# Causal mask by row tiles of 32 columns, and a new order of steps, in the first attention stage of a two-layer gated model

## The chip, the core and the metric

One Trainium2 chip, of which the program uses one core. The core has TensorE (matmuls, 128x128 array, 32-row or 32-column tiles of it can be used by themselves), VectorE, ScalarE and GpSimd, and SyncE, whose queue issues all DMAs here. The engines run their own instruction streams and meet at semaphores. The metric is the device time of one execution in microseconds.

## The reference

Two layers of gated cross attention and gated feed-forward, on x of 8 batches x 256 rows x 512. Each stage adds its result, times the tanh of a gate, to x. Only what the change touches is spelled out:

```python
# stage A: 16 heads of 32; key and value are both the context; causal
scores = jnp.einsum('bhqd,bhkd->bhqk', q, kj) * SCALE
scores = jnp.where(k_off > q_idx, -jnp.inf, scores)
exp_c = jnp.exp(scores - scores.max(axis=-1, keepdims=True))
out = jnp.einsum('bhqk,bhkd->bhqd', exp_c / exp_c.sum(-1, keepdims=True), vj)
...
x = x + jnp.tanh(g_xattn[0]) * _L0_xattn_ref(_layernorm(x), ctx, ctx)
x = x + jnp.tanh(g_ffn[0])   * _L0_ffn_ref(_layernorm(x), w_gate_up, w_proj)   # ternary weights, groups of 64
x = x + jnp.tanh(g_xattn[1]) * _L1_xattn_ref(_layernorm(x), ctx, q_w, ..., norm_k_img_w)
x = x + jnp.tanh(g_ffn[1])   * _L1_ffn_ref(_layernorm(x), w_norm, w_gv, w_out) # ternary weights, one scale
```

## The kernel before

X, the state of all eight batches, lies in on-chip memory from first to last. The work is in stages: A (L0 attention), B (L0 feed-forward, with products `b_gate_up` and `b_project`), and then C and D interleaved (L1 attention and L1 feed-forward). The change touches stage A and the step into stage B.

Stage A takes a batch per turn, in eight turns, as a software pipeline written out by hand for each engine. In a turn TensorE does this for batch b, with e = b-1 (its end) and f = b+1 (its front):

- `a_scores(b, g)`, g = 0..3: the scores of four heads, query rows on partitions, in banks 0 to 3. First the mask: one matmul per bank of the identity (128x128, bf16) with the mask (0 or -1e30, `maskS`), 256 columns, which fill the two diagonal corners of the bank. Then the products of queries and keys (L428), in four 32-row tiles, one head in each. VectorE reduces each group to maxima (L1339, `a_scores`). After two groups `a_max_parts` splits them into two bf16 parts (`a_mhl`), TensorE turns them (`a_max_turn`, L437) and VectorE copies the rows (`a_max_rows`, L1355, `a_mtr`).
- `a_probs(b, g)`: the same scores with keys on partitions, in banks 4 to 7: mask (`maskT`, L450), products (L454), and the maxima subtracted by a matmul with a selector (L459). ScalarE takes the exponential (L987).
- `a_weigh` and `a_sum` (L475, L487): the weighted values and the sums, in 32-column tiles, banks 4 and 5, for two groups at a time ("half"). `a_turn_sums`, `a_turn_out` and `a_turn_x` (L412) are transposes; VectorE divides and adds to X (`a_divide`, `a_add_out`), normalises (`stats`, `normed`), ScalarE copies the turned x to QT (`a_queries`).
- `a_project(turn, b, i)`, i = 0..3 (L517, L520): keys and values of L1 for the same context, f32, four matmuls and for the keys a bias; ScalarE copies them out, SyncE stores them to device memory.
- `a_group_sum` (L528): sums of the magnitudes of L0's feed-forward weights over groups of 64, three units a turn, banks 2 and 3. ScalarE makes magnitudes and signs before it (`a_signs`) and means after it (`a_group_mean`), VectorE rounds to ternary (`a_distance`, `a_ternary`, and for the first 16 units a maximum, L1403). `a_abs_sum` on ScalarE gathers the magnitudes of L1's weights.

Eight banks are shared by `Ring`: each has a list of who uses it in a turn, and `freed(name, turn)` gives the semaphore that the user before raises. After the turns, `m_weights` (L612, L614) spreads a maximum and sums over partitions, for which VectorE makes `m_in` at the end of its last turn (L1484); its results set the scales that the second `b_gate_up` waits for. Turn 0 (the start) loads constants, x, keys and weights in SyncE's order, makes the first projections and turns x.

The ring of bank 1, as an example of what a later step waits for:

```python
Ring([banks[1]], scores_of(0) + [("ot2", s.a_otr, 3, 0, 2)] + scores_of(2) + kv[1]),
```

Of the kernel before, what the change touches and what calls it, by code (L numbers as in the profile page):

```python
# [6 lines left out]
ALU = mybir.AluOpType  # L7
ACT = mybir.ActivationFunctionType
F32 = mybir.dt.float32
# [29 lines left out]
    ld_cst ld_x0 ld_x1 ld_kt0 ld_kt1 ld_rv0 ld_rv1 ld_w00 ld_w01 ld_w02 ld_w1a ld_w1b ld_wk ld_wv ld_sel ld_wqo ld_kb ld_row ld_wn  # L39
# [108 lines left out]
def build(nc, x, ctx, ctxT, gates, w0, w1, wkv, wqo, vec, wnorm, cols, cst, selq, selc, out):  # L148
    with ExitStack() as stack:
# [16 lines left out]
        def area(a, plan):  # L166
# [6 lines left out]
                           ("block", (P,), BF16), ("maskS", (P,), BF16), ("maskT", (P,), BF16), ("selq", (2, P), BF16), ("count", (2, DH), F32),  # L173
# [5 lines left out]
        pre = area(W0[:, :].bitcast(F32), [("cst", (4 * P,), F32), ("selq", (2 * P,), F32), ("selc", (4 * P,), F32)])  # L179
# [19 lines left out]
        late = 1  # L199
        def scores_of(first):  # L200
            return [(f"sc{g}", s.a_scr, 4, g, late) for g in (first, first + 1)]

        def probs_of(j, first):
            return [(f"pr{g}", s.a_ex, 16, 4 * g + j, late) for g in (first, first + 1)]
# [7 lines left out]
                 Ring([banks[4]], [("pv1", s.a_pvr, 2, 1, 2)] + probs_of(0, 0) + [("pv0", s.a_pvr, 2, 0, late)] + kv[0] + probs_of(0, 2)),  # L212
# [3 lines left out]
        bank_of_kv = (4, 1, 6, 7)  # L216
# [71 lines left out]
        def sync_program(sp):  # L288
# [120 lines left out]
        def tensor_program(pe):  # L409
# [7 lines left out]

            def a_scores(b, g):
                QT, KT = (bufA[n][:, b % 2 * KD + g, :] for n in ("QT", "KT"))
                pe.wait_ge(s.a_xtr, 2 * b + 2)  # L420
                pe.wait_ge((s.ld_kt0, s.ld_kt1)[b % 2], 16 * (b // 2 + 1))
                for j in range(4):
                    pe.wait_ge(*ringA[j].freed(f"sc{g}", b + 1))
                for j in range(4):
                    pe.matmul(corners(banks[j]), keep["identb"], doubled(bufA["maskS"]), start=True, stop=False, skip_group_check=True)
# [14 lines left out]
            def a_probs(b, g):  # L440
# [3 lines left out]
                if (b, g) == (0, 0):  # L444
                    pe.wait_ge(s.const, 2)
                if (b, g) == (NB - 1, 2):
                    pe.wait_ge(s.b_xl, 2)
                for j in range(4):
                    pe.wait_ge(*ringA[4 + j].freed(f"pr{g}", b + 1))
                    pe.matmul(corners(banks[4 + j]), keep["identb"], doubled(bufA["maskT"]), start=True, stop=False, skip_group_check=True)  # L450
# [5 lines left out]
                for kb in range(TB):  # L456
                    at, q0 = kb * S, kb * P
                    for j in range(4):
# [50 lines left out]
            def a_project(turn, b, i):  # L509
                what, t = i // TB, i % TB  # L510
                bank = banks[bank_of_kv[i]]
# [3 lines left out]
                pe.wait_ge(*ringA[bank_of_kv[i]].freed(f"kv{i}", turn))  # L515
# [15 lines left out]
            pe.wait_ge(s.const, 1)  # L531
            def b_turn_x(f):
                for t in range(TB):
# [3 lines left out]
                    else:  # L537
                        to = banks[6 + t]
                        pe.wait_ge(*ringA[6 + t].freed(f"xt{t}", NB))
# [3 lines left out]
            def b_gate_up(b, p, parts=(0, 1)):  # L543
# [11 lines left out]
                for part_ in parts:  # L555
                    bank, col, done = banks[first + part_], part_ * HID + 2 * p * P, (s.b_g, s.b_gu)[part_]
                    for i in range(2):
# [4 lines left out]
                    mm.then_inc(done, 1)  # L562

            a_project(0, 0, 0)
# [1518 lines left out]
```

## Time and profile before

| | us |
|---|---|
| median of 3 runs | 1184.49 (1184.33 to 1187.55) |
| the profiled execution | 1191.87 |
| its span | 1190.1 |
| TensorE busy, matmuls | 1125.8 (95%) |
| VectorE busy | 831.8 (70%) |
| ScalarE busy | 567.5 (48%) |
| start to scores 0 of turn 1 | 26.3 |
| turns 1 to 8, to the second gate product | 26.3 to 336.0 |

The span is the stretch from the first to the last instruction in the hardware's trace. A row of the timeline gives the start and the length of a run of like instructions; a matmul's length includes its way through the array, so a row of matmuls reaches past the start of the next. What a group costs TensorE is the distance from its start to the start of the next group. A number in brackets is idle time of the engine, with what ended it. Line numbers are those of the kernel before; of the changed kernel they are its own.

### The profile page before, as it was taken

The numbers are of one execution on the slowest core, as the hardware profiler recorded it, in microseconds if no ns is written. First come the engines' busy times: TensorE is split into PE (matmuls) and PEld (weight loads), VectorE is DVE, ScalarE is ACT, GpSimd is POOL, SyncE is SP. The second block draws the span as 40 slices with busy tenths as digits, with TensorE's granted clock in tenths as the row PEclk, the third lists the DMA queues.
The fourth block names the chain that finished last, engine by engine and source line by source line (L and its number), as shares of the span: only waits on it lengthen the run. The fifth ranks groups of instructions, "written<-read, shape, count | busy, mean of one in ns | idle before, by whom it ended". The sixth has DMA issues, their size and how long they took to land.

```text
span 1190.1 us, 23943 instructions
## 1 busy us (share of the span) xinstructions
PE 1125.8 (95%) x9578; PEld 686.0 (58%) x9672; DVE 831.8 (70%) x1440; ACT 567.5 (48%) x918; POOL 74.1 (6%) x180
## 2 busy tenths in 40 slices
PE   5899999999899999999999999899999999999998
PEld 2455555555577777777777655445454545454543
DVE  3677777666866765755666566778787878777785
ACT  3565666656443332333333343437373737372654
POOL 0000000000000000000000110110101010101010
PEclk9999999999999999999999999999999999999899
DMA  8554445441321201111101021000101010100000
GB/s 298 201 170 138 142 139 187 161 130 67 107 63 36 63 19 36 54 36 36 54 19 36 18 81 37 3 35 20 35 6 49 2 53 2 36 11 10 10 10 36
DMA packets 28973, 78.75 MB, mean 66 GB/s; under 512 B 3008, under 2 KB 3136, under 8 KB 28480
## 3 DMA queue, kind: packets, MB, share of 16 engines
q1 hardware_dynamic: 28864, 77.22, 19.8%
q8 instruction: 78, 1.28, 0.5%
q14 instruction: 31, 0.25, 0.1%
HBM read 64.63 MB, written 12.58 MB: 65 GB/s over the span
## 4 chain that ended last, share of the span: by engine, by line
PE 81%; DVE 9%; issue 4%; ACT 3%; another core or an unknown queue 2%; DMA 0%; SPq 0%; POOL 0%; ACTq 0%; DVEq 0%; POOLq 0%
PE bank L560 9%; PE bank L561 9%; PE bank L648 9%; PE bank L628 9%; PE bank L751 8%; PE bank L517 6%; PE bank L739 5%; PE bank L412 5%; PE bank L781 5%; DVE ARENA L1339 3%; PE bank L720 3%; PE bank L701 3%; PE bank L454 2%; PE bank L428 2%
## 5 line engine op out<-in xcount | busy, mean ns | idle before, releaser
L560 PE MATMUL bank<-ARENA,W 128*128 128x256 f16 x1024 | 228.6, 274 | 0.9 <-issue 0.9
L561 PE MATMUL bank<-ARENA,W 128*128 128x256 f16 x1024 | 228.7, 274 | 0.0
L956 ACT ACTIVATE ARENA<-bank 128x512 f32<-128x512 f32 (+3 forms) x143 | 92.8, 688 | 117.8 <-PE bank L412 39.2
L517 PE MATMUL bank<-ARENA 128*128 128x512 f32 x256 | 121.6, 620 | 10.6 <-DMA ARENA<-in_wkv 9.8
L751 PE MATMUL bank<-W,ARENA 128*128 128x512 bf16 x493 | 116.9, 383 | 2.5 <-issue 0.7
L628 PE MATMUL bank<-W,ARENA 128*128 128x512 bf16 x472 | 114.8, 379 | 3.1 <-DVE ARENA L1371 0.9
L648 PE MATMUL bank<-ARENA 128*128 128x512 f32 x256 | 116.8, 599 | 0.0
L560 PEld LDWEIGHTS bank<-ARENA,W 128*128 128x128 bf16 x1024 | 100.6, 98 | 19.7 <-issue 1.2
L561 PEld LDWEIGHTS bank<-ARENA,W 128*128 128x128 bf16 x1024 | 100.5, 98 | 18.4
L1519 DVE SCALAR_TENSOR_TENSOR ARENA<-bank,ARENA 128x512 f32<-128x512 f32 x64 | 48.0, 750 | 79.3 <-PE bank L561 78.2
L956 ACT ACTIVATE ARENA<-ARENA 128x512 f16<-128x512 f32 x64 | 40.3, 630 | 130.9 <-DVE ARENA L1519 128.1
L1144 ACT ACTIVATE ARENA<-bank,ARENA 128x512 f32<-128x512 f32 x64 | 43.7, 685 | 113.8 <-PE bank L751 106.5
L1339 DVE TENSOR_REDUCE ARENA<-bank 128x4 f32<-128x512 f32 x64 | 58.2, 951 | 52.1 <-PE bank L428 52.1
L1933 POOL TENSOR_TENSOR ARENA<-ARENA 128x2 f32<-128x2 f32 (+1 forms) x72 | 48.8, 677 | 722.4 <-DVE ARENA L1329 479.7
L751 PEld LDWEIGHTS bank<-W,ARENA 128*128 128x128 bf16 x512 | 49.1, 99 | 66.6 <-issue 12.3
L517 PEld LDWEIGHTS bank<-ARENA 128*128 128x128 f32 x256 | 48.6, 197 | 65.1 <-issue 54.0
L1065 ACT ACTIVATE ARENA<-bank 128x512 f32<-128x512 f32 x64 | 38.2, 596 | 99.1 <-PE bank L561 99.0
L1590 DVE RECIPROCAL ARENA<-bank 128x256 f32<-128x256 f32 x32 | 56.2, 1757 | 37.4 <-PE bank L739 37.3
L1559 DVE TENSOR_REDUCE ARENA<-bank 128x4 f32<-128x1024 f32 x64 | 75.2, 1218 | 6.7 <-PE bank L701 6.7
L628 PEld LDWEIGHTS bank<-W,ARENA 128*128 128x128 f16 x512 | 49.9, 99 | 49.4 <-issue 2.8
L1525 DVE TENSOR_TENSOR ARENA<-ARENA 128x512 f16<-128x512 f32 x64 | 44.3, 692 | 47.2 <-ACT ARENA L956 47.2
L648 PEld LDWEIGHTS bank<-ARENA 128*128 128x128 f32 x256 | 46.6, 190 | 52.3 <-issue 51.2
(178 smaller groups left out, 1801.5 us busy)
## 6 DMA issues: line engine op xcount, KB each, us to landing
W<-in_w SPq DMA_DIRECT2D x48, 512.0 KB, 3.8
ARENA<-in_w SPq DMA_DIRECT2D x24, 512.0 KB, 3.6
kv_store<-ARENA SPq DMA_DIRECT2D x32, 256.0 KB, 3.1
W<-kv_store SPq DMA_DIRECT2D x15, 512.0 KB, 4.5
X<-in_x SPq DMA_DIRECT2D x8, 512.0 KB, 4.7
ARENA<-in_ctxT SPq DMA_DIRECT2D x8, 512.0 KB, 3.8
ARENA<-in_ctx SPq DMA_DIRECT2D x8, 512.0 KB, 4.4
out<-X SPq DMA_DIRECT2D x16, 256.0 KB, 3.0
```

Source lines behind the costliest of these rows:

```text
L412: mm = pe.transpose(to[:, k * P:(k + 1) * P], tile, one)
L517: mm = pe.matmul(bank, bufA["KT"][:, b % 2 * KD + k, t * P:(t + 1) * P], W[:, k, :], start=(k == 0), stop=(k == KD - 1 and what == 1))
L560: pe.matmul(bank[:, i * S:(i + 1) * S], W0[:, at:at + P], xt_half(b, 0)[:, k, :], start=(k == 0), stop=False)
L561: mm = pe.matmul(bank[:, i * S:(i + 1) * S], W0[:, at:at + P], xt_half(b, 1)[:, k, :], start=False, stop=(k == KD - 1))
L628: mm = pe.matmul(banks[6 + t], hx(q, what)[:, i * S + t * P:i * S + (t + 1) * P], W0[:, UP_AT + m * D:UP_AT + (m + 1) * D], start=(m == 0 ...
L648: pe.matmul(to, src[:, k, t * P:(t + 1) * P], WQ[w][:, k, :], start=(k == 0), stop=False)
L739: mm = pe.matmul(part(to, j)[:, what * S:(what + 1) * S], lhs, bufC["PT"][:, h % 8, kb * S:(kb + 1) * S], start=(kb == 0), stop=True, skip ...
L751: mm = pe.matmul(to, QQ[d][:, t, k * P:(k + 1) * P], W1[:, at:at + D], start=(k == 0), stop=(k == KD - 1))
L781: mm = pe.matmul(to, UT[d, t][:, k * P:(k + 1) * P], W1[:, UP_AT + k * D:UP_AT + (k + 1) * D], start=(k == 0), stop=(k == KH - 1))
L956: return act.activation(to, src, ACT.Copy)
L1339: got = v.tensor_reduce(NM[:, t, :, g % 2], bank[:, 0:4, t * P:t * P + (t + 1) * P], AX_X, ALU.max, negate=True)
L1559: got = v.tensor_reduce(NM[:, t, :, g], bank[:, 0:4, t * S:(t + 1) * S], AX_X, ALU.max, negate=True)
```

## The change

Parts:

1. The mask matmul is cut into strips. `a_mask` puts four strips of 32 mask columns (twice, for the two corners: 64 columns) into each of four banks, each strip with a matmul that uses 32 rows of the array: the stationary operand is a 32 x 128 part of the mask, stored in another layout (`maskS`, `maskT` are now 4 x 128 per partition, loaded as `masks`, 512 KB, by a DMA of its own), the moving one a 32 x 32 part of the identity, read twice. 16 matmuls of 64 columns instead of 4 of 256, for each of the 64 blocks.
2. TensorE's order in a turn is new; ScalarE's and VectorE's follow. `project(b,3)` moves ahead of the group sum of unit 1, `project(f,0)` ahead of probs 1, the turning out and `a_weigh(b,0)` between scores 2 and 3; VectorE does distance and ternary of unit 1 ahead of the reduction of scores 2. Key and value products 0 and 1 both use bank 1, and the exponentials go through banks 6, 7, 4, 5 in this order.
3. The start: keys, weights of the key projection and the bias come first in SyncE's queue, x and constants after. VectorE makes `ones` and zeros first, TensorE runs ten matmuls on zeros, then both key products of batch 0, then the transposes. VectorE splits the bias before it takes x's statistics.
4. The last turn: stage B's first transposes go to banks 1 and 0 and stand between probs 0 and probs 1, the first gate products are split in halves (`sides`), and `m_weights` stands ahead of probs 3. `b_project` of batch 0 waits for as many ternary units as it needs, not for all.

```diff
+def strip(bank, m):
+    return corners(bank)[:, :, m * DH:(m + 1) * DH]
...
-                 Ring([banks[1]], scores_of(0) + [("ot2", s.a_otr, 3, 0, 2)] + scores_of(2) + kv[1]),
+                 Ring([banks[1]], scores_of(0) + [("ot2", s.a_otr, 3, 0, 2)] + kv[0] + scores_of(2) + kv[1]),
...
-            sp.dma_start(pre["cst"], cst).then_inc(s.ld_cst, 16)
-            load_x(0)
             load_keys(0)
...
+            load_x(0)
+            sp.dma_start(pre["cst"], cst).then_inc(s.ld_cst, 16)
...
+            sp.dma_start(pre["masks"], masks).then_inc(s.ld_sel, 16)
...
+            def a_mask(to, mask):
+                for m in range(4):
+                    for j in range(4):
+                        one = part(keep["identb"], j)[:, j * DH:(j + 1) * DH]
+                        pe.matmul(strip(to[j], m), part(mask, j)[:, m, :], doubled(one), start=(m == 0), stop=False, skip_group_check=True)
...
-                for j in range(4):
-                    pe.matmul(corners(banks[j]), keep["identb"], doubled(bufA["maskS"]), start=True, stop=False, skip_group_check=True)
+                a_mask(banks[0:4], bufA["maskS"])
...
+                if (b, g) == (NB - 1, 2):
+                    pe.wait_ge(s.b_xl, 2)
...
+            for n in range(10):
+                pe.matmul(banks[7], bufA["MHL"][:, 0, :], bufA["MHL"].rearrange("p a b -> p (a b)"), start=True, stop=True)
+            a_project(0, 0, 0)
+            a_project(0, 0, 1)
+            pe.wait_ge(s.const, 2)
+            a_turn_x(0, 0)
...
+                a_scores(b, 1)
+                if end:
+                    a_sum(turn, e, 1)
+                    a_project(turn, b, 3)
+                a_group_sum(turn, b, 1)
+                a_max_turn(turn, b, 0)
+                if end:
+                    a_turn_sums(turn, e)
+                a_probs(b, 0)
+                a_group_sum(turn, b, 2)
+                if front:
+                    a_project(turn, f, 0)
+                else:
+                    b_turn_x(0)
+                a_probs(b, 1)
+                a_scores(b, 2)
+                if end:
+                    a_turn_out(turn, e)
+                a_weigh(turn, b, 0)
+                a_scores(b, 3)
+                a_sum(turn, b, 0)
...
+                    m_weights()
+                    b_gate_up(0, 0, (1,), (0,))
+                a_probs(b, 3)
...
                 if back:
+                    a_distance(b, 1)
+                    if not front:
+                        b_turn_x(0)
+                    a_ternary(b, 1)
                     a_scores(b, 2)
-                    a_distance(b, 1)
```

How the instructions stand. On TensorE in the middle of an ordinary turn (turn 5), from the mask of scores 1 (L425 before, L433 after) to the turning of the sums (L412, L423). Before:

```order
L425 MATMUL bank<-ARENA 128x2x128 x4
L428 MATMUL bank<-ARENA 128x128 x4
L428 MATMUL bank<-ARENA 128x256 x4
L487 MATMUL bank<-ARENA 32x256 x4
L487 MATMUL bank<-ARENA 32x128 x4
L487 MATMUL bank<-ARENA 32x256 x4
L487 MATMUL bank<-ARENA 32x128 x4
L528 MATMUL bank<-W,ARENA 128x512 x2
L517 MATMUL bank<-ARENA 128x512 x4
L437 MATMUL bank<-ARENA 128x128 x2
L528 MATMUL bank<-W,ARENA 128x512 x2
L412 MATMUL bank<-ARENA,W 128x128 x4
```

After (L537 is the projection, L548 the group sum, L457 the turning of the maxima):

```order
L433 MATMUL bank<-ARENA 128x2x32 x16
L448 MATMUL bank<-ARENA 128x128 x4
L448 MATMUL bank<-ARENA 128x256 x4
L505 MATMUL bank<-ARENA 32x256 x4
L505 MATMUL bank<-ARENA 32x128 x4
L505 MATMUL bank<-ARENA 32x256 x4
L505 MATMUL bank<-ARENA 32x128 x4
L537 MATMUL bank<-ARENA 128x512 x4
L548 MATMUL bank<-W,ARENA 128x512 x2
L457 MATMUL bank<-ARENA 128x128 x2
L423 MATMUL bank<-ARENA,W 128x128 x4
```

The projection has moved ahead of the group sum, the second group sum is gone from here (it comes after probs 0), and the mask's matmuls are 16 narrow ones.

On SyncE at the start of the program, before:

```order
L323 DMA W<-in_cst 128x512
L292 DMA X<-in_x 128x2x512
L298 DMA ARENA<-in_ctxT 128x1024
L326 DMA ARENA<-in_gates 128x4
L327 DMA ARENA<-in_cols 128x12
L328 DMA ARENA<-in_wkv 128x2048
L329 DMA ARENA<-in_vec 128x512
```

After (the first four rows are keys, key weights, bias and x):

```order
L308 DMA ARENA<-in_ctxT 128x1024
L334 DMA ARENA<-in_wkv 128x2048
L335 DMA ARENA<-in_vec 128x512
L302 DMA X<-in_x 128x2x512
L337 DMA W<-in_cst 128x256
L338 DMA ARENA<-in_gates 128x4
L339 DMA ARENA<-in_cols 128x12
L320 DMA W<-in_w 128x1024
L341 DMA ARENA<-in_wkv 128x2048
L342 DMA W<-in_masks 128x1024
```

Keys, weights and bias come before x and the constants; the masks are a load of their own behind the value weights.

On TensorE at the end of turn 8, from the mask of probs 3, before (L612 and L614 are `m_weights`):

```order
L450 MATMUL bank<-ARENA 128x2x128 x4
L454 MATMUL bank<-ARENA 128x256 x4
L454 MATMUL bank<-ARENA 128x128 x4
L459 MATMUL bank<-ARENA 128x256 x4
L459 MATMUL bank<-ARENA 128x128 x4
L612 MATMUL bank<-W,ARENA 32x128 x4
L614 MATMUL bank<-ARENA 32x24 x4
```

And after, from the mask of probs 2 (L589 and L591 are `m_weights`, L579 and L580 a gate product):

```order
L433 MATMUL bank<-ARENA 128x2x32 x16
L472 MATMUL bank<-ARENA 128x256 x4
L472 MATMUL bank<-ARENA 128x128 x4
L477 MATMUL bank<-ARENA 128x256 x4
L477 MATMUL bank<-ARENA 128x128 x4
L589 MATMUL bank<-W,ARENA 32x128 x4
L591 MATMUL bank<-ARENA 32x24 x4
L579 MATMUL bank<-ARENA,W 128x256
L580 MATMUL bank<-ARENA,W 128x256
```

`m_weights` has moved from behind probs 3 to right behind probs 2, and a quarter of the first gate products follows it.

## Rows read from the trace of the kernel before

**Rows 1.** The page: busy time and share by engine; the chain's shares.

```profile
PE 1125.8 (95%) x9578; PEld 686.0 (58%) x9672; DVE 831.8 (70%) x1440; ACT 567.5 (48%) x918; POOL 74.1 (6%) x180
...
PE 81%; DVE 9%; issue 4%; ACT 3%; another core or an unknown queue 2%; DMA 0%; SPq 0%; POOL 0%; ACTq 0%; DVEq 0%; POOLq 0%
```

**Rows 2.** Windows: stretch: us, busy us (instructions) per engine, granted clock, DMA share, GB/s.

```profile
9.80:13.20 3.40, 3.37 (x4) 1.51 (x5) 2.35 (x8) 0.00 (x0) 0.69 (x1) 1.00 1.05 422
37.20:40.50 3.30, 3.30 (x6) 1.24 (x5) 1.34 (x5) 2.91 (x3) 0.69 (x1) 0.50 0.48 170
54.00:282.00 228.00, 216.00 (x2292) 124.28 (x2303) 164.47 (x282) 140.98 (x246) 4.14 (x6) 1.00 0.46 147
```

**Rows 3.** Timeline of TensorE, turns 2 to 4: start, us, instructions [idle before <-releaser].

```profile
65.02 0.61 PE L425 MATMUL bank<-ARENA 128*128 128x256 bf16 x4
...
140.92 0.34 PE L459 MATMUL bank<-ARENA 32*128 32x256 bf16 x8
141.19 0.61 PE L425 MATMUL bank<-ARENA 128*128 128x256 bf16 x4
141.74 0.94 PE L428 MATMUL bank<-ARENA 32*128 32x128 f32 x16
...
146.34 1.51 PE L475 MATMUL bank<-ARENA 128*32 128x256 f32 x32
...
151.75 0.38 PE L528 MATMUL bank<-W,ARENA 128*128 128x512 bf16 x1 [1.05 <-DVE ARENA L1339]
...
155.39 0.27 PE L437 MATMUL bank<-ARENA 128*128 128x128 bf16 x2
...
161.69 0.60 PE L425 MATMUL bank<-ARENA 128*128 128x256 bf16 x4 [0.55 <-DVE ARENA L1339]
```

**Rows 4.** The same view, end of the stage and the late transposes: short matmuls.

```profile
329.01 0.24 PE L614 MATMUL bank<-ARENA 128*32 128x24 f32 x8
329.18 0.28 PE L560 MATMUL bank<-ARENA,W 128*128 128x256 f16 x1
...
1128.63 1.06 PE L412 MATMUL bank<-ARENA 128*128 128x128 bf16 x16
```

**Rows 5.** Timelines of VectorE and of ScalarE, turn 4.

```profile
149.57 1.81 DVE L1339 TENSOR_REDUCE ARENA<-bank 128x4 f32<-128x512 f32 x2
...
155.77 0.29 DVE L1355 COPY ARENA<-bank 128x256 bf16<-128x256 bf16 x1 [2.29 <-PE bank L437]
...
158.16 1.62 ACT L987 ACTIVATE ARENA<-bank 128x384 f32<-128x384 f32 x4
...
167.60 1.09 ACT L956 ACTIVATE ARENA<-bank 128x512 f32<-128x512 f32 x2 [0.17 <-PE bank L412]
```

**Rows 6.** Timelines of TensorE and of VectorE, from the start to probs 0.

```profile
9.83 5.37 PE L517 MATMUL bank<-ARENA 128*128 128x512 f32 x8 [9.83 <-DMA ARENA<-in_wkv]
15.81 0.39 PE L520 MATMUL bank<-ARENA 128*128 128x512 bf16 x1 [0.60 <-DVE ARENA L1417]
...
42.95 0.61 PE L450 MATMUL bank<-ARENA 128*128 128x256 bf16 x4
...
12.65 0.42 DVE L1408 CAST ARENA<-ARENA 128x512 bf16<-128x512 f32 x1
...
27.86 1.82 DVE L1339 TENSOR_REDUCE ARENA<-bank 128x4 f32<-128x512 f32 x2 [11.45 <-PE bank L428]
...
34.70 1.81 DVE L1339 TENSOR_REDUCE ARENA<-bank 128x4 f32<-128x512 f32 x2
```

**Rows 7.** Timelines of TensorE and of VectorE, turn 8 and the step into stage B.

```profile
293.61 0.61 PE L425 MATMUL bank<-ARENA 128*128 128x256 bf16 x4
...
335.97 0.27 PE L560 MATMUL bank<-ARENA,W 128*128 128x256 f16 x1 [0.85 <-issue]
...
321.87 0.28 DVE L1355 COPY ARENA<-bank 128x256 bf16<-128x256 bf16 x1
...
326.30 0.29 DVE L1484 TENSOR_SCALAR W<-ARENA 128x128 f32<-128x128 f32 x1
```

More of the change, by code:

```diff
@@ L145, in corners, with build @@
     return bank[:, 0:2 * S].rearrange("p (a b) -> p a b", a=2)[:, :, 0:P]
-def build(nc, x, ctx, ctxT, gates, w0, w1, wkv, wqo, vec, wnorm, cols, cst, selq, selc, out):
+def strip(bank, m):
+    return corners(bank)[:, :, m * DH:(m + 1) * DH]
+def build(nc, x, ctx, ctxT, gates, w0, w1, wkv, wqo, vec, wnorm, cols, cst, masks, selq, selc, out):
     with ExitStack() as stack:
@@ L199, in build @@
         late = 1
+        by_bank = (2, 3, 0, 1)
         def scores_of(first):
@@ L203, in probs_of @@
         def probs_of(j, first):
-            return [(f"pr{g}", s.a_ex, 16, 4 * g + j, late) for g in (first, first + 1)]
+            return [(f"pr{g}", s.a_ex, 16, 4 * g + by_bank.index(j), late) for g in (first, first + 1)]
         kv = [[(f"kv{i}", s.a_kvr, 4, i, late * (i // 2))] for i in range(4)]
@@ L457, in a_probs @@
                     at, q0 = kb * S, kb * P
-                    for j in range(4):
+                    for j in by_bank:
                         mm = pe.matmul(banks[4 + j][:, at:at + S - q0], part(SEL, j), part(MT, j)[:, q0:S], start=False, stop=True,
@@ L556, in b_gate_up @@
                     bank, col, done = banks[first + part_], part_ * HID + 2 * p * P, (s.b_g, s.b_gu)[part_]
-                    for i in range(2):
+                    for i in sides:
                         for k in range(KD):
@@ L784, in d_out_product @@
                     mm.then_inc(s.d_y, 1)
-            m_weights()
             for b in range(NB):
@@ L1029, in scalar_program @@
                 a_signs(b, 2)
+                if end:
+                    a_abs_sum(b, 0)
                 a_projected(b, 2)
@@ L1440, in vector_program @@
                     stats(0, s.b_ve)
+                if turn == 0:
+                    v.wait_ge(s.ld_cst, 16)
+                    v.tensor_copy(keep["identf"], pre["cst"][:, 0:P])
+                    v.tensor_copy(keep["identb"], pre["cst"][:, 0:P])
+                    v.tensor_copy(bufA["block"], pre["cst"][:, P:2 * P]).then_inc(s.const, 1)
                 if back:
@@ L1470, in vector_program @@
                     a_max_parts(b, 1)
-                    a_ternary(b, 1)
-                    if not front:
-                        b_turn_x(0)
                     a_max_rows(b, 1)
@@ L2039, in arrays_of @@
     mask_s = np.where(r[None, :] > r[:, None], NEG, 0.0).astype(np.float32)
+    strips = [np.tile(m.T.reshape(4, DH, P).transpose(1, 0, 2), (4, 1, 1)).reshape(P, 4 * P) for m in (mask_s, mask_s.T)]
     selq = np.zeros((P, 2, P), np.float32)
@@ L2061, in arrays_of @@
         "wnorm": np.broadcast_to(f["L1_ffn_w_norm"], (P, D)),
-        "cst": np.concatenate([eye, block, mask_s, mask_s.T], axis=1),
+        "cst": np.concatenate([eye, block], axis=1),
+        "masks": np.concatenate(strips, axis=1),
         "cols": np.concatenate(cols, axis=1),
```

181 lines of the change are left out of this document (83 added, 98 removed).

## The prediction

> **What bounds the kernel now.** Three views, in this order: the page's totals and chain, the windows over the middle of the attention stage, and the timeline of TensorE over one turn.
>
> The page shows a kernel bound by TensorE: its matmuls are busy for 95% of the span and make up 81% of the chain that ended last [rows 1]. The change touches only the first 324 us (L0 attention); what follows keeps its instructions and is TensorE's own work, so a microsecond gained before it is a microsecond at the end. The window over six turns, 54 to 282 us, says how much is to be had there: 216.0 us busy of 228, so 12 us idle, 2.0 us in each turn, at full clock, with VectorE busy for 27.4 us and ScalarE for 23.5 us of a turn (164.5 and 141.0 over six) [rows 2]. Neither is the bound.
>
> The timeline shows where the turn's time goes [rows 3]. Scores of group 0 start at 65.02 and, two turns later, at 141.19: a turn is 38.1 us. The idle pieces: 1.05 us before the group sum at 151.75, which needs banks 2 and 3, still being reduced by VectorE since 149.57 (1.81 us, [rows 5]); 0.55 us before the scores at 161.69, the same wait; and about 0.3 us before `probs(b,2)`: 1.9 us. The rest, 36.2 us, is instructions, eight mask blocks among them. A mask block is four matmuls of 256 columns: (0.61 - 0.28) / 3 = 0.11 us apart, four are 0.44 us, and the next block starts 0.55 us after it (141.19 to 141.74). The 0.11 us over is what it costs to go from a full-array matmul to one in 32-row tiles. The L459 block shows the same on the way back: eight matmuls in four row tiles stream 256 + 128 columns (0.16 us) and take 0.27 us until L425 starts (140.92 to 141.19).
>
> **The masks.** Four matmuls of 256 columns per block become 16 of 64 columns in four row tiles, hence four rounds. No row shows this form. The lower bound is the nearest short one: the eight L614 matmuls (24 columns, 32-wide tiles, two rounds of four) have 0.17 us to themselves (329.01 to 329.18), 0.11 of which is the change of tiling, so 0.03 us a round and 0.12 us a block [rows 4]. From above: 16 bf16 transposes, each with a load of 128 columns, take 1.06 us, the last 0.22 of it its own drain; 0.056 us each [rows 4]. A round that pays such a load once costs 0.056, a block 0.22. If the load of one round can't lie beside the matmuls of the others, it is worse, and that is a rival. I take 0.18, between the two, nearer the transposes, since the load of 128 columns is what the strips have: 0.44 - 0.18 = 0.26 us a block, 2.1 us a turn. In the new order two mask blocks follow a 32-row block directly and all of them lead into one; counted along the program, a turn changes tiling 16 times instead of 21, five times 0.11: 0.6 us. Masks: 2.7 us a turn, 0.6 from below if a block stays at 0.44, 3.2 from above at 0.12.
>
> **The order of the turn.** (1) `project(b,3)`, 3.43 us, now stands between the scores of group 1 and the group sum. It covers the reduction of 1.8 us: the 1.05 us goes. (2) `weigh(b,0)` and the turning out now stand between the scores of groups 2 and 3, 2.4 us; on VectorE distance and ternary of u=1 move ahead of the group-2 reduction, 3.9 us of work (5.1 with the maximum) that starts after the reciprocals, about 1.3 us after `probs(b,0)` starts, plus 1.3 us of `a_add_out`: 6.5 to 7.7 us. TensorE meanwhile has probs 0, a group sum, a projection, probs 1 and scores 2 (1.3 + 0.4 + 3.6 + 1.3 + 1.0), 7.6 us: VectorE is free just when the scores are there. The 0.55 us goes, and the divide (1.3 us) is ready before `turn_x`. (3) `project(f,0)` moves up between probs 0 and probs 1, where it hides the four exponentials (1.62 us, [rows 5]). What is late next: before `probs(b,0)` only `turn_sums` (0.43 us) lies behind `max_turn`, whose rows need 0.38 us to reach VectorE and 0.29 us to be copied (155.39 to 155.77, [rows 3, 5]): a new gap of 0.3. Behind `turn_x` there is no projection any more, only `max_turn` and a group sum, 0.55 us, while ScalarE copies the second query half, half of the 1.09 us of [rows 5], after 0.2 us on the way and behind the first: 0.3. The maximum parts of half 1 arrive 0.1 late. New waits: 0.7 us. ScalarE's queue behind each is an exponential group or the mean of a group, which have a projection's 3.6 us of slack. SP's program after the start is unchanged; its store of `kv(f,0)` still stands behind a load that waits for `signs(f,1)`, so it gains nothing and loses nothing, and the next user of that buffer is 10 us later. Keys of the next batch land some 10 us before the projection that is now earlier.
>
> A turn: 38.1 - 1.9 - 2.7 + 0.7 = 34.2 us. Turns 2 to 7: 6 x 3.9 = 23.4 us.
>
> **The start and turn 1.** Keys, the key half of wkv and vec come first, without cst (0.25 MB) and x (0.5 MB) ahead; at 422 GB/s [rows 2] that is 1.9 us earlier than the 9.83 of [rows 6], when this half of wkv had come: the first projection at 7.9. The ten dummy matmuls from 1.4 us on should have the clock up before. Its bias needs vec (8.6) and six operations of VectorE, 3.15 us (12.65 to 15.8, where L520 waited for them): 11.8. The second projection follows at full clock (3.6 instead of the 5.37 of the first one before) to 15.5, `turn_x` to 16.5, `project(0,2)` after the first query copy 17.3 to 20.7, scores 0 to 21.9. The masks (0.5 MB more in the queue, landed by about 15.7, copied by 17.5) are in time. Then the chain is VectorE's, as before: there the first reduction ran from 27.86 and the second from 34.70 [rows 6], 6.85 us apart; now 22.0 and 28.9, ending 30.7, then max parts, statistics and copy: `probs(0,0)` at 33.3 instead of 42.95, 9.6 us. That includes the half-clocked projection of [rows 2] at 37.2 to 40.5, now moved ahead. From there to the next turn it was 22.1 us (42.95 to 65.02), and now 34.2 - 13.4 - 1.0 = 19.8 (13.4 is what stands ahead of probs 0 in a turn, 15.2 before less 1.05, two blocks and a change of tiling, more the 0.2 or 0.3 of the new gap; 1.0 the turning out, of which there is none yet), plus 1.7 for one stretch at half clock after the 4 us wait for the reduction: 21.5. Together 10.2 us.
>
> **Turn 8.** From scores 0 (293.61) to the second gate product (335.97) 42.4 us [rows 7]. Now `b_turn_x` is early, but `scores(7,2)` waits for its low halves, which sit on VectorE behind distance: 2.4 us idle. `m_weights` stands ahead of gate product part 1 and `probs(7,3)` and needs `m_in`, which came 4.7 us after the last copy of maxima (321.87 to 326.6, [rows 7]); TensorE has only probs 2 (1.3) there: 3 us idle. Stepping through with the rows' durations: the copy at 28.3 us of the turn, `m_in` 33.1, probs 3 to 35.9, exponentials to 37.5, weigh and sum to 40.4, reciprocals 42.0, second gate product 42.1. Gain 0.3 us, within -1.5 to 2: the masks' saving ends in VectorE's chain.
>
> **Sum.** 23.4 + 10.2 + 0.3 = 33.9 us. The profiled execution took 1191.87 us (span 1190.1), so 1158.0; the median of the runs is 7.4 us below it, 1184.49 - 33.9 = 1150.6. Forecast 1151.
>
> **Rivals.** (1) A strip costs its weight load. The L614 round of 0.03 us loads 32 columns; if a load costs by the column and isn't hidden, a strip's round is 0.12, a block 0.46 and no shorter than before. For it: nothing in the trace shows bf16 loads into row tiles that aren't covered. Against it: the transposes' 0.056 us. Then only 0.5 us a turn is left of the 2.7, 8 x 2.2 = 17.6 us less: 1168.
> The Trainium skill speaks for it twice, in TensorE: Matmul & The Clock Gate. Its section LDWEIGHTS (loading the stationary operand) has a load last its columns over 1.2, "a 32×128 weight load takes the same time as a 128×128 weight load": 107 ns a round, 0.43 a block. Its section Wait — 56ns, not 53.3ns? has starts never closer than about 25 ns however few the columns: 0.40 a block. By either the time would be an estimated 1165 to 1167. The L614 row, eight matmuls in 0.06 us net, disagrees with the second across tiles; no run here shows the first.
> (2) The waits only move. If the 2.0 us of a turn come back, behind VectorE's longer run ahead of the group-2 reduction or the query copies, 6 x 1.3 = 8 us are lost: 1159. For it: the 1 us margin in (2) above. Against: VectorE would still be idle for 7 us of 34.
> (3) Slower: TensorE's supply of instructions. A turn has 96 more load-and-matmul pairs. Without the block's 2.1 us a turn 17 us of gain remain, 0.27 us for each of the 64 blocks, so a block longer than 0.71 us, 45 ns a strip, makes the change a loss. The 32 pairs of L475 take 1.51 us [rows 3], at most 47 ns each, so this form of row does not exclude it; if the strips ran one after the other at the 0.11 us of today's, a block were 1.74 us and the time 1184 - 17 + 64 x 1.3 = 1250. Against it: the L614 row again. (4) The change does not reach the end: the start's gain is taken by the loads that now land 1 us later and a half-clocked stretch per turn appears: about 1180.
>
> **Chances.** Forecast 60%, own range 1144 to 1158. Rival 1 15%, rival 2 17%, rival 3 5%, rival 4 3%. Range 1141 to 1169: it takes in rivals 1 and 2, the bounds of the mask block (0.12 us: 4 us less), and leaves out 3 and 4 and the tails. A difference of 0.3%, 3.6 us, is what can be told from none: faster 0.93, the same 0.02, slower 0.05.
>
> **What would show it.** Right: scores 0 of turn 5 to those of turn 6 in 34 us; a mask block to the first score product in 0.2 to 0.3 us (the full-array matmul ahead of it included); no idle before the group sums; `probs(0,0)` near 33 us; idle before `m_weights` of about 3 us. Wrong: mask blocks of 0.4 us and more (rival 1 or 3), turns of 36 us with idle before the scores of group 3 or probs 2 (rival 2), a second gate product that is more than 2 us earlier or later in its turn.

## The result, and the profile after

| | before | after | forecast |
|---|---|---|---|
| median, same chip | 1185.83 (4 runs, 1184.33 to 1187.55) | 1154.47 (4 runs, 1152.59 to 1157.88) | 1151 |
| ratio to before, 95% interval | | 0.9738 [0.9708, 0.9769] | 0.972 |
| the profiled execution, its span | 1191.87, 1190.1 | 1155.84, 1154.0 | 1158.0 |
| start to scores 0 of turn 2 | 65.0 | 56.1 (-8.9) | -10.2 |
| turns 2 to 7 | 228.6 | 201.1 (-27.5) | -23.4 |
| turn 8, scores 0 to the second gate product | 42.4 | 45.8 (+3.4) | -0.3 |
| the rest of the program | 854.1 | 851.0 (-3.1) | 0 |

Faster by 31.4 us by the medians, where 33.9 was forecast. The three terms of the change sum to -33.0. The fourth row is not the change's work. In the rest of the program the profiled execution before is at half clock for 13.6 us (3.4 us at 764.2, 6.8 at 1105.5, 3.4 at 1170.3) and the one after for 6.8 (3.4 at 731.3, 3.4 at 1134.0):

```profile
1105.50:1112.30 6.80, 6.68 (x58) 3.40 (x60) 2.23 (x6) 4.22 (x5) 0.00 (x0) 0.50 0.00 0
```

6.8 us less at half clock are 3.4 us of time, against 3.1 measured. Two executions can differ in this by a few us: in the profiled ones of experiments 4 and 8 the rest of the program has no such stretch at all and takes 849.1 us. So what a step is worth is read below from its own stretch of the trace, and the medians only say whether it is seen at the end. One execution of experiment 1 (1657.23 us, mean granted clock 0.65) was disturbed and is in no median.

The page after, to be set against [rows 1]:

```profile
PE 1112.5 (96%) x10450; PEld 672.7 (58%) x10450; DVE 833.0 (72%) x1440; ACT 566.9 (49%) x918; POOL 74.2 (6%) x180
...
PE 90%; DVE 5%; ACT 2%; issue 2%; DMA 1%; POOL 0%; ACTq 0%; SPq 0%; DVEq 0%; POOLq 0%
```

TensorE's share of the chain that ended last rose from 81% to 90%, which is 75 us more of the span on TensorE (964 to 1039) where the span fell by 36. So that chain also runs another way through the program, and its shares are no measure of the gain. The windows (stretch: us, busy us and instructions of PE, PEld, DVE, ACT, POOL, granted clock, DMA share, GB/s), over the turns and over two stretches that matter below:

```profile
50.00:250.00 200.00, 199.07 (x2876) 112.66 (x2876) 164.27 (x281) 140.09 (x245) 4.13 (x6) 1.00 0.54 170
7.00:11.10 4.10, 4.08 (x6) 1.78 (x7) 3.21 (x7) 0.21 (x1) 0.00 (x0) 0.58 1.08 408
...
291.00:297.80 6.80, 6.30 (x72) 4.24 (x72) 2.49 (x17) 1.55 (x4) 0.00 (x0) 0.50 0.01 2
```

The third row is read with turn 8 below. In the turns 0.93 us of 200 is idle by this view, against 12 of 228 in [rows 2]; VectorE still has 18% to spare. TensorE's timeline of a turn (start, us, instructions, idle before it) answers to [rows 3]:

```profile
123.06 0.30 PE L433 MATMUL bank<-ARENA 32*128 32x64 bf16 x16
123.17 0.92 PE L448 MATMUL bank<-ARENA 32*128 32x128 f32 x16
...
131.50 3.70 PE L537 MATMUL bank<-ARENA 128*128 128x512 f32 x8
135.03 0.59 PE L548 MATMUL bank<-W,ARENA 128*128 128x512 bf16 x2
...
135.58 0.61 PE L423 MATMUL bank<-ARENA,W 128*128 128x128 f32 x4
136.20 0.30 PE L433 MATMUL bank<-ARENA 32*128 32x64 bf16 x16
...
148.50 1.09 PE L423 MATMUL bank<-ARENA 128*128 128x128 f32 x8
149.59 0.27 PE L457 MATMUL bank<-ARENA 128*128 128x128 bf16 x2
149.72 0.59 PE L548 MATMUL bank<-W,ARENA 128*128 128x512 bf16 x2
150.48 0.30 PE L433 MATMUL bank<-ARENA 32*128 32x64 bf16 x16 [0.17 <-ACT ARENA L989]
...
156.65 0.30 PE L433 MATMUL bank<-ARENA 32*128 32x64 bf16 x16
```

(The rows of 148.50 to 149.72 are read under "Why the prediction was right".) Scores 0 start 33.6 us apart (123.06, 156.65), 33.5 on the mean of the turns. A block of strips lets the products start 0.11 us later (123.06 to 123.17), not 0.55; no group sum waits; the only wait that the view shows is 0.17 us before probs 2.

The start, against [rows 6]:

```profile
1.23 3.81 PE L596 MATMUL bank<-ARENA 128*128 128x512 bf16 x10 [1.23 <-DVE ARENA L1339]
7.03 5.40 PE L537 MATMUL bank<-ARENA 128*128 128x512 f32 x8 [1.99 <-DMA ARENA<-in_wkv]
12.26 0.38 PE L540 MATMUL bank<-ARENA 128*128 128x512 bf16 x1
...
21.17 0.29 PE L433 MATMUL bank<-ARENA 32*128 32x64 bf16 x16
...
31.07 0.59 PE L548 MATMUL bank<-W,ARENA 128*128 128x512 bf16 x2 [4.28 <-DVE ARENA L1367]
...
33.29 0.40 PE L433 MATMUL bank<-ARENA 32*128 32x64 bf16 x16 [1.43 <-DVE ARENA L1383]
```

`probs(0,0)` starts at 33.29, where 33.3 was forecast; the dummies (L596) end 2 us before the first projection, which runs at half clock from 7.7 on and takes 5.40 us, not 3.6.

Turn 8, against [rows 7]:

```profile
273.47 0.30 PE L433 MATMUL bank<-ARENA 32*128 32x64 bf16 x16 [0.53 <-ACT ARENA L1020]
...
277.23 0.37 PE L433 MATMUL bank<-ARENA 32*128 32x64 bf16 x16 [2.55 <-issue]
...
288.29 0.33 PE L477 MATMUL bank<-ARENA 32*128 32x256 bf16 x8
291.50 0.66 PE L589 MATMUL bank<-W,ARENA 128*32 128x128 f32 x8 [2.88 <-DVE W L1522]
...
301.49 0.63 PE L423 MATMUL bank<-ARENA,W 128*128 128x128 f32 x4 [0.65 <-ACT W L989]
302.97 0.27 PE L579 MATMUL bank<-ARENA,W 128*128 128x256 f16 x1 [0.85 <-issue]
```

Two waits are new: 2.55 us before scores 2 (277.23), and 2.88 us before `m_weights` (L589, 291.50), which stands ahead of probs 3. Around the end of each wait the granted clock falls to half, for 3.4 us from 277.3 and for 6.8 us from 291.0. Turn 8 of the kernel before had one wait of more than 1 us, 2.00 us long (before probs 2, 322.21) and one such stretch, 3.4 us from 323.8.

### The profile page after: what moved, and what is told of

It reads as the page before. It is cut to its first block, busy times and chain, and to the rows that moved or that the text cites. A ratio compares the mean times of both kernels' runs of the same rounds, so it can differ in the third digit from the quotient of the medians.

```text
span 1154.0 us, 25637 instructions
## 1 busy us (share of the span) xinstructions
PE 1112.5 (96%) x10450; PEld 672.7 (58%) x10450; DVE 833.0 (72%) x1440; ACT 566.9 (49%) x918; POOL 74.2 (6%) x180
## 4 chain that ended last, share of the span: by engine, by line
PE 90%; DVE 5%; ACT 2%; issue 2%; DMA 1%; POOL 0%; ACTq 0%; SPq 0%; DVEq 0%; POOLq 0%
PE bank L537 10%; PE bank L579 10%; PE bank L580 10%; PE bank L662 10%; PE bank L682 9%; PE bank L785 8%; PE bank L773 5%; PE bank L423 5%; PE bank L815 5%; PE bank L735 3%; PE bank L754 3%; PE bank L472 2%; PE bank L493 2%; PE bank L505 2%; PE bank L448 2%
## 5 line engine op out<-in xcount | busy, mean ns | idle before, releaser
L579 PE MATMUL bank<-ARENA,W 128*128 128x256 f16 x1024 | 228.7, 274 | 1.6 <-issue 1.6
L580 PE MATMUL bank<-ARENA,W 128*128 128x256 f16 x1024 | 228.7, 274 | 0.0
L989 ACT ACTIVATE ARENA<-bank 128x512 f32<-128x512 f32 (+3 forms) x143 | 92.9, 689 | 86.3 <-PE bank L423 31.4
L537 PE MATMUL bank<-ARENA 128*128 128x512 f32 x256 | 120.3, 614 | 2.0 <-DMA ARENA<-in_wkv 2.0
L662 PE MATMUL bank<-W,ARENA 128*128 128x512 bf16 x512 | 121.0, 379 | 0.7 <-DVE ARENA L1399 0.7
L785 PE MATMUL bank<-W,ARENA 128*128 128x512 bf16 x512 | 119.6, 383 | 0.7 <-DVE W L1697 0.3
L579 PEld LDWEIGHTS bank<-ARENA,W 128*128 128x128 bf16 x1024 | 100.5, 98 | 20.8 <-issue 2.3
L580 PEld LDWEIGHTS bank<-ARENA,W 128*128 128x128 bf16 x1024 | 100.5, 98 | 18.2
L989 ACT ACTIVATE ARENA<-ARENA 128x512 f16<-128x512 f32 x64 | 40.3, 630 | 130.9 <-DVE ARENA L1557 128.1
L785 PEld LDWEIGHTS bank<-W,ARENA 128*128 128x128 bf16 x512 | 49.2, 99 | 66.3 <-issue 11.8
L1367 DVE TENSOR_REDUCE ARENA<-bank 128x4 f32<-128x512 f32 x64 | 58.3, 952 | 38.6 <-PE bank L448 38.4
L537 PEld LDWEIGHTS bank<-ARENA 128*128 128x128 f32 x256 | 47.8, 194 | 57.4 <-issue 53.9
```

The source lines that it names most:

```text
L537: mm = pe.matmul(bank, bufA["KT"][:, b % 2 * KD + k, t * P:(t + 1) * P], W[:, k, :], start=(k == 0), stop=(k == KD - 1 and what == 1))
L579: pe.matmul(bank[:, i * S:(i + 1) * S], W0[:, at:at + P], xt_half(b, 0)[:, k, :], start=(k == 0), stop=False)
L580: mm = pe.matmul(bank[:, i * S:(i + 1) * S], W0[:, at:at + P], xt_half(b, 1)[:, k, :], start=False, stop=(k == KD - 1))
L662: mm = pe.matmul(banks[6 + t], hx(q, what)[:, i * S + t * P:i * S + (t + 1) * P], W0[:, UP_AT + m * D:UP_AT + (m + 1) * D], start=(m == 0 ...
L785: mm = pe.matmul(to, QQ[d][:, t, k * P:(k + 1) * P], W1[:, at:at + D], start=(k == 0), stop=(k == KD - 1))
L989: return act.activation(to, src, ACT.Copy)
```

## Experiments

The theory after the result: the strips take 0.42 us out of each of 64 blocks, all of it on TensorE's path; the order removes the idle time and by itself is worth little; the load order is worth the start; and the step that was forecast wrongly is turn 8, through `m_weights`. Rivals: the strips' price is hidden in something else; order and strips only pay together; the dummies, not the loads, made the start.

**1. The new order with the old masks.**

```diff
-                for m in range(4):
-                    for j in range(4):
-                        ... strip(to[j], m), part(mask, j)[:, m, :], doubled(one) ...
+                for j in range(4):
+                    pe.matmul(corners(to[j]), keep["identb"], doubled(mask[:, 0, :]), start=True, ...)
```

> The changed kernel with the mask put in as before: four matmuls of the whole identity with 256 columns per bank group instead of 16 strips; order, start and end stay new. Theory (the parts add up): the order alone takes the idle 1.9 us out of a turn, the strips alone 0.42 us out of each of the 64 blocks (0.54 before, 0.12 after), less some tenths of waits that come free: turns of 36.5 to 36.9 us instead of 33.5, the time 1154.5 + 8 x 3.2 = 1180 (1174 to 1182), still faster than the kernel before by the start's 9 us less the 3 us of turn 8. Rival (the order does it all): within 4 us of 1154.5. Rival (the strips do it all): at 1186 or above.

(The mask's layout in memory is changed to match.) 1178.62 us (1178.0 to 1179.13), ratio 0.9918 [0.9887, 0.9948]. Without the strips only 0.8% of the 2.6% is left, and this is what the new order, the new start and the new last turn give together: the strips are worth 1.8% on top of them (0.9918 to 0.9738), 24 us by the medians. Its turns are read in experiment 10.

**2. The strips in the order of before.** The same `a_mask`, mask layout and load of its own, put into the kernel before; nothing else. (The masks' load stands behind the first feed-forward weights and ahead of the value weights, not behind these.)

> The kernel before with the mask strips alone; masks as a load of their own behind the value weights. Order, start and end as before. Theory: in the old order part of the strips' 0.42 us per block turns into waits for VectorE's reductions (ahead of the group sum and of scores 3) and for ScalarE's exponentials (ahead of probs 1), which follow a fixed time after the shortened blocks: turns of about 36.4 us with idle of 3 us or more, the time 1186 - 8 x 1.7 = 1172 (1166 to 1177). Rival (strips and order are independent): turns of 34.9, time 1160. Rival (strips pay only in the new order): 1183 or more.

1174.63 us (1172.71 to 1175.7), ratio 0.9884 [0.9857, 0.9911]. A block takes 0.115 us here too, so eight take 3.4 us less, but turns are 36.4 to 36.5 us, only 1.6 shorter. The timeline of TensorE in one turn shows where the rest is:

```profile
136.52 3.67 PE L529 MATMUL bank<-ARENA 128*128 128x512 f32 x8 [0.52 <-ACT ARENA L999]
...
145.07 0.38 PE L540 MATMUL bank<-W,ARENA 128*128 128x512 bf16 x1 [1.03 <-DVE ARENA L1351]
...
153.25 0.30 PE L427 MATMUL bank<-ARENA 32*128 32x64 bf16 x16 [1.27 <-ACT ARENA L999]
...
156.02 1.09 PE L417 MATMUL bank<-ARENA 128*128 128x128 f32 x8 [0.72 <-ACT ARENA L999]
...
165.32 0.30 PE L427 MATMUL bank<-ARENA 32*128 32x64 bf16 x16 [0.25 <-DVE ARENA L1367]
```

3.8 us idle in the turn, where [rows 3] add up to 1.9. Half of the strips' gain turned into waits, some of them for ScalarE (L999 is the exponential), which the old order had covered only because TensorE was slower. So in the old order the strips are worth 1.6 us a turn. What the new order, start and last turn are worth together, 0.8% without the strips (experiment 1), is 1.5% with them (0.9884 to 0.9738).

**3. Every strip twice.**

```diff
-                for m in range(4):
+                for n in range(8):
+                    m = n % 4
```

> The changed kernel with every strip of every mask put in twice (the mask value doubles, which changes no result): 16 more matmuls and weight loads in each of 64 blocks. It measures a strip by itself. Theory: a round of four strips costs 0.03 us, so a block 0.12 more, the time 64 x 0.12 = 7.7 us more, 1162. If a round costs its load as in a transpose (0.056): 14 us more, 1169. If load and supply cost 0.1 a round: 26 us more, 1180.

1163.98 us (1161.84 to 1164.81), ratio 0.9793 [0.9761, 0.9826]. TensorE's timeline at scores 1:

```profile
130.79 0.41 PE L434 MATMUL bank<-ARENA 32*128 32x64 bf16 x32
131.03 0.95 PE L449 MATMUL bank<-ARENA 32*128 32x128 f32 x16
```

32 strips take 0.24 us and 16 take 0.13; turns are 34.73 instead of 33.5, so 0.154 us for a doubled block and 0.04 for one of its four rounds. That excludes the rival in which a round waits for its load. The loads are not short: in the trace after, a load of 32 rows by 128 columns lasts 93 ns (the median of 928), nearly what a load of the whole array does (98 ns, L425 before). The Trainium skill, TensorE: Matmul & The Clock Gate, section LDWEIGHTS (loading the stationary operand), gives both the same length, 107 ns, and for the length of one load the trace agrees but for some 10 ns. But a whole round of four, loads included, adds only 40 ns, so the loads of different tiles lie beside each other, and the length of one is not the price of a round.

**4. `m_weights` behind the turns again.**

```diff
                 else:
-                    m_weights()
                     b_gate_up(0, 0, (1,), (0,))
...
+            m_weights()
             for b in range(NB):
```

> The changed kernel with m_weights back behind probs 3 of the last turn, where it stood before. Theory: turn 8 lost time because TensorE waits 2.9 us at m_weights for VectorE, and falls to half clock after it; with it behind probs 3 the gate product and probs 3 fill that wait and exponentials, weigh and sum come 2.5 to 4 us earlier: scores 0 of turn 8 to the second gate product 42.5 us instead of 45.8, the time 1151.5 (1150 to 1152.5). Rival: the second gate product then waits for the scales that m_weights gives, and nothing is gained, 1154.5.

1150.75 us (1148.8 to 1156.27), ratio 0.9692 [0.9656, 0.9729], an interval that still overlaps the changed kernel's, so the gain is shown by the trace and not by the times. Turn 8 is 41.25 us (256.90 to 298.15) instead of 45.8, and its timeline shows why:

```profile
288.14 0.28 PE L579 MATMUL bank<-ARENA,W 128*128 128x256 f16 x1
...
290.14 0.30 PE L433 MATMUL bank<-ARENA 32*128 32x64 bf16 x16 [0.96 <-ACT ARENA L1020]
...
291.27 0.42 PE L589 MATMUL bank<-W,ARENA 128*32 128x128 f32 x8
...
293.22 1.51 PE L493 MATMUL bank<-ARENA 128*32 128x256 f32 x32 [0.49 <-ACT ARENA L1020]
```

`m_weights` no longer waits; in its place are a wait of 0.96 us before probs 3 and one of 0.49 before `a_weigh` (293.22), and the stretch at half clock is gone. The first wait of the turn, 2.55 us, and its stretch of 3.4 us are still there. Of the 4.5 us that the turn gains, 1.4 is waiting (2.88 less 0.96 and 0.49) and 3.1 the half clock: the stretch of 6.8 us held 6.30 us of matmuls at half speed.

**5. The loads of the start in the old order.** `cst` and x go ahead of keys, gates and wkv again; the products stay in the new order.

> The changed kernel with SyncE's first loads in the old order (constants, x, keys, gates, columns, key weights, bias), all else new. Theory: the first projection waits for the key weights, which have 0.64 MB more ahead of them, at 422 GB/s 1.5 us later; it starts at 8.6 instead of 7.0 and all of the start moves by the same: the time 1156 (1.5 us more). Rival (the load order is worth most of the start's 9 us): 1160 or more.

1159.02 us (1157.38 to 1162.09), ratio 0.977 [0.9744, 0.9797]. The timeline of the start:

```profile
10.09 5.41 PE L537 MATMUL bank<-ARENA 128*128 128x512 f32 x8 [4.41 <-DMA ARENA<-in_wkv]
...
36.35 0.40 PE L433 MATMUL bank<-ARENA 32*128 32x64 bf16 x16 [0.98 <-DVE ARENA L1383]
```

The first projection is 3.06 us later and so is `probs(0,0)`: the 3 us of the load order pass through unchanged, twice the size expected. They are a third of the 9.7 us by which `probs(0,0)` moved (42.95 to 33.29), so the rival, that the load order is worth most of the start, fails too, though the time comes near its 1160. The other 6.6 us come with the new order of the products, the cheaper masks and VectorE's new order in the start; no run separates these.

**6, 7. No dummies, and sixteen.**

```diff
-            for n in range(10):
+            for n in range(0):      # 6; range(16) in 7
                 pe.matmul(banks[7], bufA["MHL"][:, 0, :], ...)
```

> The changed kernel without its ten matmuls on zeros. Theory: they run from 1.2 to 5.0 us, the clock is up from 4.3 and falls at 7.7, because TensorE is idle from 5.0 to 7.0; the first projection runs at half clock with them (5.2 us) and will without them: no difference, 1154.5 within 1.5, the first projection 5.2 to 6.9 us. Rival (they help, as meant): the first projection takes all of 6.9 us and the time is 1156 or more.

> The changed kernel with 16 matmuls on zeros instead of ten, until about 6.4 us. Theory: the idle ahead of the first projection is then 0.6 us instead of 2.0, the clock stays up, the first projection takes 3.6 us less what the bias makes it wait (VectorE has it at 10.8, so its bias matmul starts at 10.8 instead of 12.3): everything until turn 1 comes 1.5 us earlier, 1153. Rival: the clock still falls, 1154.5.

Without: 1155.92 us, ratio 0.9737 [0.9716, 0.9759]. The first projection starts at 6.90 and takes 5.77 us, its bias follows at 12.50 instead of 12.26: the ten change nothing that can be measured in the time. Sixteen: 1155.39 us, ratio 0.9732 [0.9706, 0.9757], no gain either, though they do what they are for:

```profile
1.23 6.04 PE L596 MATMUL bank<-ARENA 128*128 128x512 bf16 x16 [1.23 <-DVE ARENA L1339]
7.10 3.60 PE L537 MATMUL bank<-ARENA 128*128 128x512 f32 x8
...
29.47 0.59 PE L548 MATMUL bank<-W,ARENA 128*128 128x512 bf16 x2 [4.27 <-DVE ARENA L1367]
...
32.08 0.40 PE L433 MATMUL bank<-ARENA 32*128 32x64 bf16 x16 [1.90 <-ACT ARENA L989]
```

The projection runs at full clock (3.60 us) and scores 0 come at 19.57, 1.6 us earlier. VectorE's chain begins with the scores, so the group sum behind it is 1.6 earlier too (29.47 instead of 31.07). But `probs(0,0)` now waits for a copy of ScalarE's (L989) and gains 1.2, and turn 2 starts 0.7 earlier (55.41), which does not show in the time. The theory of 1153 was wrong: more than half of the gain is given back between the group sum and turn 2.

**8. Experiment 4, and x of stage B turned earlier in turn 8.** On ScalarE its copies go ahead of the group mean and the sum of magnitudes, on VectorE its low halves ahead of distance.

```diff
                 if back:
+                    if not front:
+                        b_turn_x(0)
                     a_distance(b, 1)
-                    if not front:
-                        b_turn_x(0)
                     a_ternary(b, 1)
```

> The changed kernel with m_weights behind probs 3 and, in the last turn, the copies and low halves of stage B's first x taken ahead of the group mean and magnitude sum on ScalarE and ahead of distance on VectorE. Theory: scores 2 of turn 8 wait for the low halves, which ScalarE's queue holds up by 2 us: idle of 0.5 us instead of 2.55 there, the last turn 39.5 us to the second gate product instead of 45.8 (41.3 with m_weights alone), the time 1149 (1147.5 to 1150.5). Rival: VectorE's chain to the maxima of half 1 is the same, as distance comes later by as much, and nothing is gained over m_weights alone, 1151.

1150.66 us (1148.49 to 1151.13), ratio 0.9691 [0.9669, 0.9714]. Turn 8 takes 40.0 us, another 1.2 less, which the medians don't tell apart from experiment 4. The waits moved on:

```profile
275.76 0.30 PE L433 MATMUL bank<-ARENA 32*128 32x64 bf16 x16 [0.74 <-ACT W L1006]
...
281.36 0.30 PE L433 MATMUL bank<-ARENA 32*128 32x64 bf16 x16 [1.65 <-DVE ARENA L1367]
```

0.74 us before scores 2 instead of 2.55, but 1.65 before scores 3, for the reduction of scores 2. The granted clock is full throughout turn 8.

**9. Experiment 8, and one step of VectorE moved in turn 1.**

```diff
                     a_distance(b, 0)
-                    a_ternary(b, 0)
+                    if b > 0:
+                        a_ternary(b, 0)
                     a_scores(b, 1)
...
+                    if b == 0:
+                        a_ternary(b, 0)
                     a_distance(b, 1)
```

> The kernel with m_weights behind the turns and x turned earlier in turn 8, and on top of it one step of VectorE moved in turn 1 alone: ternary of unit 0 (0.69 + 0.69 + 1.22 us, 24.0 to 29.1 together with distance) goes behind the normalisation of x, so that the reduction of scores 1, which started at 29.11 while the scores were there at 26.8, starts at 27.0. Theory: TensorE's 4.27 us wait before the group sum at 31.08 shrinks to 2.2, probs(0,0) start at 31.2 instead of 33.3, turn 2 at 54 instead of 56.1, and the time is 1148.6, 2 us below the 1150.7 of the kernel without this step. Rival: as with the six dummy matmuls more (1.6 us earlier at scores 0, 0.7 left at turn 2), the gain is taken by what ScalarE and the store of kv release next: probs(0,0) earlier by 2 but turn 2 at 55.5 or later, time 1150 to 1151.

1148.47 us (1145.46 to 1149.04), ratio 0.968 [0.9661, 0.9698].

```profile
28.77 0.59 PE L548 MATMUL bank<-W,ARENA 128*128 128x512 bf16 x2 [2.05 <-DVE ARENA L1367]
...
31.02 0.30 PE L433 MATMUL bank<-ARENA 32*128 32x64 bf16 x16 [1.56 <-DVE ARENA L1383]
```

The wait fell from 4.27 to 2.05 us and `probs(0,0)` came 2.3 earlier, as the theory has it; turn 2 starts at 52.98, 3.1 earlier. Of the 0.8 beyond the 2.3, 0.5 lies right behind `probs(0,0)` (2.42 us to the next projection instead of 2.92), where the stretch at half clock is 3.4 us long now, not 6.8. With experiment 7 this shows what bounds turn 1 from scores 0 to `probs(0,0)`: VectorE's chain, which begins with the scores and has the reduction of scores 1 near its end, not TensorE's products beside it. It is the fastest kernel of the study; against the changed kernel's ratio of 0.9738 [0.9708, 0.9769] its interval lies wholly below, against experiment 8's the intervals overlap.

**10. Experiment 1's kernel once more, for its turns.**

> The new order with full-array masks once more, for a profile of its turns alone (the time is known: 1178.6). Theory (the order by itself removes the 2 us of idle, the masks lie on TensorE's path): turns of 36.1 to 36.5 us, busy for all but 0.2 us of each, a mask block 0.53 to 0.55 to the next start. Rival (part of the order's gain came only together with the strips): idle of 1 us or more per turn in this kernel, turns of 37 us and more.

Turns of 36.8 us (95.37, 132.19, 169.01), by two rows of TensorE's timeline and its window:

```profile
132.19 0.61 PE L431 MATMUL bank<-ARENA 128*128 128x256 bf16 x4
...
162.14 0.60 PE L431 MATMUL bank<-ARENA 128*128 128x256 bf16 x4 [0.16 <-ACT ARENA L987]
```

```profile
54.00:270.00 216.00, 215.06 (x2251) 120.91 (x2253) 160.55 (x275) 138.18 (x241) 4.15 (x6) 1.00 0.49 153
```

By the view the idle time is gone as the theory has it (0.94 us of 216), yet the turn is 0.3 to 0.7 us longer than it expected: TensorE is busy for 36.6 us of a turn (215.06 / 216 x 36.8), where it was for 36.1 (216.0 / 228 x 38.1, [rows 2]). The 0.5 us are no added work; the next section finds them. The rival is refuted: the idle time went without the strips. The order alone is worth 38.1 - 36.8 = 1.3 us a turn, and the strips on top of it 36.8 - 33.5 = 3.3 = 8 x 0.41.

## Why the prediction was right

Its mechanism was right in the turns, and its time is 0.3% off; that it is so near is partly luck, since two errors of 4 and 5 us cancel. By its own steps:

- *What bounds.* Right: an instruction off TensorE's path in a turn is time off the end.
- *Masks, 2.7 us a turn.* 3.3 (experiments 1, 10). A block is 0.12 to 0.13 us, the forecast's lower bound, and 0.18 was taken because of the loads of 128 columns in the late transposes. The L614 row, with tiles, was the nearer one; the transposes use the whole array. 8 x 0.05 makes 0.4 of the 0.6 us.
- *Idle time -1.9, new waits +0.7.* Right, net (1.2, where experiment 10 measured 1.3) and in its parts, though the view hides most of the new waits: a row's length includes the matmuls' way through the array, which covers a short wait behind them. By the distances of starts three waits are new or left in the turn shown. Before `probs(b,0)`: the sums' transposes take 0.62 us (135.58 to 136.20), which took 0.43 before (155.94 to 156.37) and take 0.62 with the old masks too (experiment 10), so it is not the strips; the mask starts 0.06 us after VectorE has copied the rows (135.85 + 0.29), as it does at 33.29, where the view names that copy. Before `a_max_turn`: 0.16 us (the transposes of x take 1.09 us from 148.50, and took 0.93, 166.85 to 167.78); VectorE's second part ends at 149.45 and L457 starts at 149.59. Before probs 2: 0.32 us (0.76 from the group sum's start, 0.44 its own), of which the view shows 0.17. Together 0.67 us, where 0.3, 0.1 and 0.3 were forecast. The old idle time by the same measure is 0.84 + 0.62 + 0.46 = 1.9: of the 1.05 us before the group sum, 0.21 is a matmul whose record is missing (L528 has 48 loads and 40 matmuls in the trace of before). Missing record and covered waits are the 0.5 us of experiment 10. TensorE before, then VectorE after:

```profile
155.94 0.60 PE L412 MATMUL bank<-ARENA,W 128*128 128x128 f32 x4
156.37 0.60 PE L450 MATMUL bank<-ARENA 128*128 128x256 bf16 x4
...
166.85 1.09 PE L412 MATMUL bank<-ARENA 128*128 128x128 f32 x8
167.78 3.60 PE L517 MATMUL bank<-ARENA 128*128 128x512 f32 x8
```

```profile
135.85 0.29 DVE L1383 COPY ARENA<-bank 128x256 bf16<-128x256 bf16 x1 [0.94 <-PE bank L457]
...
149.27 0.18 DVE L1378 TENSOR_TENSOR ARENA<-ARENA 128x16 bf16<-128x16 f32 x1
```

- *Rival 1, load by the column.* Refuted (experiment 3), and *rival 3*, a block above 0.71 us, with it. *Rival 2*, the waits only move: not with the new order, but it is what half of the strips' gain does in the old one (experiment 2), which the prediction did not foresee as a reason why both parts belong together.
- *Start and turn 1, -10.2.* -8.9. `probs(0,0)` came out at 33.29 for 33.3, by two errors that cancel: the first projection started 0.9 us earlier than thought (7.03, not 7.9), and the dummies did not keep the clock up, so that its bias came 0.5 us later (12.26, not 11.8). Behind it 22.8 us to turn 2 instead of 21.5: 5.1 us at half clock (33.29 to 38.4) cost 2.6 where 1.7 was counted, and a wait of 0.76 us before `weigh(0,0)` (44.11, for the exponentials) was not counted at all.
- *Turn 8, -0.3.* +3.4, the mis-sized term, outside its own -1.5 to 2, and one of the prediction's signs of being wrong: the second gate product came 3.7 us later in its turn than forecast, with 2 as the limit. Both waits were foreseen nearly to the size (2.4 and 3 us; 2.55 and 2.88), but not that each goes with a stretch at half clock, 10.2 us together where turn 8 before had 3.4. That holds 1.7 + 3.1 us of lost speed instead of 1.7, so 3.1 of the 3.7; no run places the rest. Experiment 4 removes the second wait and the second stretch and gets 4.5 us back.

The two misses in the turns (4.1 us too little) and at both ends (5.0 too much) nearly cancel. By the medians the gain is 31.4 us, 1.6 less than the three terms of the traces, which is within what stretches at half clock elsewhere change from one execution to the next.

## What to carry to other kernels

A cheaper instruction on the bound engine is worth its full saving only as far as the order of the work keeps other engines ahead of it: the same strips gave 1.6 us a turn in the old order and 3.3 in the new, so a speed-up and a reordering are costed together. A foreseen idle time of 2 to 3 us on TensorE is priced with the stretch at half clock behind it. And before a start is sped up, see whose chain ends it: here part of it was one vector reduction behind 2.6 us of work that could wait.

## What the runs showed of the hardware

- 16 matmuls of 32 rows by 64 columns in four row tiles, each with its load of 32 x 128, take 0.12 us, and 32 take 0.24: 7.5 ns each, though the record of one such load is 93 ns long (median). Loads and matmuls of different tiles lie beside each other.
- The clock fell to half around the end of waits of 2.55 and 2.88 us in turn 8 (for 3.4 and 6.8 us), of 2.00 in turn 8 of the kernel before (3.4 us), and of 2.05 and 1.56 in turn 1 (experiment 9, 3.4 us), and stayed full in turn 8 with waits of 0.74, 1.65 and 0.96 (experiment 8).
- A wait of up to 0.2 us behind a row of matmuls does not show as idle time: 0.19 and 0.16 us in each turn did not.
- Ten warm-up matmuls that end 2 us ahead of the work buy nothing here: the clock was at half from 7.7 on, in the middle of the first projection. Sixteen that end with the load's arrival keep it full.
